# Decoder layer on one core: the feed-forward's first block of rows is split by GpSimd and projected at the end of the cross attention

## The reference, cut to what matters

```python
x = x + attn_ref(layernorm(x), w_qkv, w_out)                    # self attention, 16 heads
x = x + xattn_ref(layernorm(x), ctx, ctx, mask, Wq, bq, ..., Wo, bo)
#   q = query @ Wq.T + bq; softmax over the keys; out @ Wo.T + bo
x = x + ffn_ref(layernorm(x), index_b, index_t, sw1, sb1, ...)
#   shared part: sh = ln(silu(x1) * x2) * g + b; sh @ sw3.T + sb3 for all rows,
#   and one of 8 experts for each of 1024 chosen rows
```

## Time and profile before

| | us |
|---|---|
| median of three runs | 3107.37 |
| lowest and highest | 3104.04, 3114.0 |
| the profiled execution, its time | 3114.0 |
| the profiled execution, its span | 3112.0 |
| TensorE busy in the span | 2916.7 |
| VectorE, ScalarE, GpSimd busy | 2079.8, 1609.6, 1740.0 |
| cross attention ends, feed-forward starts (us from the span's start) | 2617.51 |
| first `up` of the feed-forward | 2639.83 |

### The profile page before, as it was taken

How to read it: one execution, slowest core, us unless ns; L and a number is a source line. 1 busy time by engine, 2 the same in 40 slices (tenths; PEclk the granted TensorE clock), 3 DMA queues, 4 the chain that set the end, 5 groups by cost and what they waited for, 6 DMA issues and landing times. The chain is left out here.

```text
span 3112.0 us, 41615 instructions
## 1 busy us (share of the span) xinstructions
PE 2916.7 (94%) x15224; PEld 1729.4 (56%) x15224; DVE 2079.8 (67%) x3794; ACT 1609.6 (52%) x2998; POOL 1740.0 (56%) x748
## 2 busy tenths in 40 slices
PE   8999799999999999999999999979969997999577
PEld 5888455555555555555555555437855554777533
DVE  4332587777777777777777777635638896677423
ACT  2222066666676666667676767733226674222211
POOL 1000178989898989898989898830020101343366
PEclk9999699999999999999999999989979998999689
DMA  6544835466566565665665656357665563333451
GB/s 224 187 170 155 217 79 119 96 140 130 117 138 130 119 135 112 134 133 113 140 127 119 133 114 144 79 146 210 186 145 141 139 158 115 136 136 109 142 189 40
DMA packets 179536, 427.52 MB, mean 137 GB/s; under 512 B 30189, under 2 KB 51598, under 8 KB 156236
## 3 DMA queue, kind: packets, MB, share of 16 engines
q1 hardware_dynamic: 153158, 275.92, 30.9%
q0 software_dynamic: 24288, 145.27, 23.0%
q10 hardware_dynamic: 1888, 3.67, 0.4%
HBM read 180.69 MB, written 118.79 MB: 96 GB/s over the span
## 5 line engine op out<-in xcount | busy, mean ns | idle before, releaser
L822 DVE TENSOR_REDUCE part_max<-ps_s 128x1 f32<-128x512 f32 x2048 | 1270.5, 684 | 369.6 <-PE ps_s L710 369.4
L924 ACT ACTIVATE probs<-ps_st 128x512 f32<-128x512 f32 x2048 | 1058.6, 603 | 493.0 <-PE ps_st L729 477.9
L657 POOL TENSOR_TENSOR added<-added,probs 128x2048 f32<-128x2048 f32 x251 | 1168.0, 4653 | 72.0 <-ACT probs L924 48.8
L729 PE MATMUL ps_st<-q_stack,k_stack 98*128 98x512 f32 x2048 | 866.6, 426 | 10.1 <-ACT probs L924 8.7
L710 PE MATMUL ps_s<-k_stack,q_stack 96*128 96x512 f32 x2048 | 825.9, 410 | 17.2 <-DMA k_stack<-k_lo 17.2
L729 PEld LDWEIGHTS ps_st<-q_stack,k_stack 98*128 98x128 f32 x2048 | 387.4, 190 | 520.4 <-ACT probs L924 368.7
L740 PE MATMUL ps_pv<-probs,v_sb 128*32 128x512 f32 x4096 | 547.2, 606 | 0.0
L710 PEld LDWEIGHTS ps_s<-k_stack,q_stack 96*128 96x128 f32 x2048 | 396.3, 194 | 111.4 <-DVE part_max L822 30.6
L665 POOL DMA_DIRECT2D probs<-probs x128 | 111.1, 868 | 181.1 <-PE ps_pv L740 176.5
L740 PEld LDWEIGHTS ps_pv<-probs,v_sb 128*32 128x32 f32 x4096 | 80.8, 108 | 162.9 <-ACT probs L924 136.8
L657 POOL TENSOR_TENSOR added<-probs 128x2048 f32<-128x2048 f32 x32 | 146.7, 4586 | 10.6 <-ACT probs L924 10.3
(11 more groups left out here) (294 smaller groups left out, 3709.1 us busy)
## 6 DMA issues: line engine op xcount, KB each, us to landing
probs<-probs POOLq DMA_DIRECT2D x128, 1024.0 KB
q_stack<-q_hi SPq DMA_DIRECT2D x64, 256.0 KB, 6.8
k_stack<-k_hi SPq DMA_DIRECT2D x64, 256.0 KB, 5.9
xq_stack<-q_parts SPq DMA_DIRECT2D x32, 512.0 KB, 5.0
q_parts<-k_stack SPq DMA_DIRECT2D x60, 256.0 KB, 4.2
x_in<-in_x_rows SPq DMA_DIRECT2D x8, 1024.0 KB
q_hi<-qk_h_out SPq DMA_DIRECT2D x8, 1024.0 KB, 4.2
q_lo<-qk_l_out SPq DMA_DIRECT2D x8, 1024.0 KB
```

The lines of the kernel that those rows point to most:

```text
L657: pool.tensor_tensor(added[:, w % 2], left, probs[:, k % RING], ALU.add).then_inc(added_up, 1)
L729: pe.matmul(ps_st[:, n % BANKS], k_stack[0:TOP, w // BPB, j, k * P:(k + 1) * P], q_stack[:, w % 4, j], start=True, stop=True).then_inc(ite ...
L822: dve.tensor_reduce(part_max[:, s:s + 1], ps_s[:, (w * SLOTS + s) % BANKS], AX.X, ALU.max)\
L924: act.activation(probs[:, k % RING, j], ps_st[:, n % BANKS], ACT.Exp, scale=SCALE).then_inc(item_used, 1)
```

## The change

GpSimd takes over the split of the first block (four casts and four subtractions, one for each chunk of 128 x 512) as soon as it is loaded, adds bo to the block's residual rows, and at the end takes the reciprocal square root for two tiles. TensorE makes the first block's 48 projection matmuls at the end of the cross attention, into the banks of `ps_s`. VectorE adds them to `next_x` in place after its last `normalize` and makes the statistics of the first two tiles between those additions. The feed-forward then starts with `norm(0, 0, 0)` and takes the first block's rows from `first_x`. Semaphores that the first block would have raised are raised by hand. bo is loaded at unit 21, and the waits of the start are for the loads that each step needs: `ident_in` for the transposes, `bias_in` for ScalarE. To make room, the second buffer of row maxima (`row_parts`) moves into unused partitions of the `probs` tile.

```diff
@@
-        probs = sb("xprobs", [KH, 2, 2, HEADS, BLK])
+        probs_all = sb("xprobs", [P, 2, 2, HEADS, BLK])
+        probs = probs_all[0:KH]
-        row_parts = [early_rows, sb("xrow_parts", [2 * HEADS, BLK], F32R)[:]]
+        row_parts = [early_rows, probs_all[96:96 + 2 * HEADS, 0, 0, 0].bitcast(F32R)]
...
+                            sp.dma_start(bo_all, bo.partition_broadcast(P)).then_inc(bo_loaded, 16)
...
+                pool.memset(next_half[:], -0.5).then_inc(ones_set, 1)
+                pool.wait_ge(ones_set, 2)
+                pool.wait_ge(next_loaded, 128)
+                for c in range(DC):
+                    pool.tensor_copy(next_h[:, c], ahead_raw[:, c // 2, c % 2]).then_inc(next_high, 1)
+                for c in range(DC):
+                    pool.wait_ge(next_high, c + 1)
+                    pool.tensor_tensor(next_l[:, c], ahead_raw[:, c // 2, c % 2], next_h[:, c].bitcast(F32), ALU.subtract)\
+                        .then_inc(next_low, 1)
+                pool.wait_ge(bo_loaded, 16)
+                for t in range(TPB):
+                    pool.tensor_tensor(next_x[:, t], next_x[:, t], bo_all, ALU.add).then_inc(bo_added, 1)
+                pool.wait_ge(next_eps_added, 1)
+                pool.tensor_tensor(next_rstd[:, 0:2], next_var[:], next_half[:], ALU.pow).then_inc(next_rstd_done, 1)
+                pool.wait_ge(next_rstd_done, 1)
...
+                def project_next(t):
+                    if t == 0:
+                        pe.wait_ge(max_done, UNITS * SLOTS)
+                        pe.wait_ge(next_low, DC)
+                        pe.wait_ge(ahead_low, 2 * len(PARTS))
+                    if t >= BANKS:
+                        pe.wait_ge(next_summed, t - BANKS + 1)
+                    a, w = (next_h, next_l), weights_ahead[0][1:]
+                    for n, (x, y) in enumerate(ORDER):
+                        for c in range(DC):
+                            mm = pe.matmul(ps_s[:, t % BANKS], a[x][:, c, t * P:(t + 1) * P], w[y][:, c],
+                                           start=(n == 0 and c == 0), stop=(n == 2 and c == DC - 1))
+                    mm.then_inc(next_projected, 1)
...
+                for t in range(TPB):
+                    project_next(t)
...
-                    if u == UNITS:
-                        dve.wait_ge(next_high, 1)
-                        dve.tensor_tensor(next_l, ahead_raw[:].rearrange("p a c d -> p (a c) d"), next_h.bitcast(F32), ALU.subtract)\
-                           .then_inc(next_low, 1)
...
+                for t in range(TPB):
+                    dve.wait_ge(bo_added, t + 1)
+                    dve.wait_ge(next_projected, t + 1)
+                    dve.tensor_tensor(next_x[:, t], ps_s[:, t % BANKS], next_x[:, t], ALU.add).then_inc(next_summed, 1)
+                    if t < 2:
+                        dve.wait_ge(next_summed, t + 1)
+                        dve.bn_stats(next_stats[:, t], next_x[:, t]).then_inc(next_stats_done, 1)
+                    if t == 1:
+                        dve.wait_ge(next_stats_done, 2)
+                        dve.sem_inc(next_stats_seen, 1)
+                        for k in range(2):
+                            dve.bn_aggr(next_moments[:, k], next_stats[:, k]).then_inc(next_moments_done, 1)
+                        dve.wait_ge(next_moments_done, 2)
+                        dve.tensor_scalar(next_var[:], next_moments[:, 0:2, 1], EPS, None, ALU.add).then_inc(next_eps_added, 1)
...
-                    if u == UNITS - 1:
-                        act.wait_ge(next_loaded, 128)
-                        act.activation(next_h, ahead_raw[:].rearrange("p a c d -> p (a c) d"), ACT.Copy).then_inc(next_high, 1)
...
-                sp.dma_start(bo_all[:], bo.partition_broadcast(P)).then_inc(bo_loaded, 16)
-                for dst, src in ((ident[:], eye), (bias_raw[:, 0:D], b12.unsqueeze(0)), (bias_raw[:, D:2 * D], b3.unsqueeze(0)),
-                                 (gamma_all[:], gamma.partition_broadcast(P)),
+                sp.dma_start(ident[:], eye).then_inc(ident_in, 16)
+                sp.dma_start(bias_raw[:, 0:D], b12.unsqueeze(0)).then_inc(bias_in, 16)
+                sp.dma_start(bias_raw[:, D:2 * D], b3.unsqueeze(0)).then_inc(bias_in, 16)
+                for dst, src in ((gamma_all[:], gamma.partition_broadcast(P)),
...
-                pool.wait_ge(bo_loaded, 16)
-                add_bias(0, 0)
-                pool.wait_ge(consts, 5)
-                pool.wait_ge(w_loaded, 5 * 16)
-                rsqrt(0, 0, 0)
+                pool.sem_inc(bo_added, TPB)
+                pool.sem_inc(rstd_done, 1)
                 rsqrt(0, 0, 1)
+                pool.wait_ge(w_loaded, 2 * 16)
...
-                residual(0, 0, range(2))
-                residual_stats(0, 0, 0)
-                residual(0, 0, (2,))
+                dve.sem_inc(resid_done, TPB)
+                dve.sem_inc(stats_done, 2)
+                dve.sem_inc(moments_done, 2)
+                dve.sem_inc(eps_added, 1)
+                norm(0, 0, 0)
+                residual_stats(0, 0, 1)
+                norm(0, 0, 1)
                 dve.wait_ge(bias_high, 1)
                 dve.tensor_tensor(bias_rows[32:33], bias_raw[:], bias_rows[0:1].bitcast(F32), ALU.subtract)\
                    .then_inc(bias_low, 1)
-                residual(0, 0, (3,))
-                norm(0, 0, 0)
-                residual_stats(0, 0, 1)
-                norm(0, 0, 1)
...
-                act.wait_ge(w_loaded, 5 * 16)
+                act.wait_ge(bias_in, 2 * 16)
...
-                project(0, 0, range(TPB))
-                pe.wait_ge(w_loaded, 5 * 16)
+                pe.sem_inc(proj_done, TPB)
+                pe.wait_ge(ident_in, 16)
```

More of the change, by code:

```diff
@@ L1280, in cross_attention @@
 def cross_attention(nc, q_parts, xk_parts, xv_rows, pad_row, pad_scaled, mask_q, mask_k, eye, eye_bf, attn_t, weights_ahead,
-                    x1_rows, next_x, next_h, next_l, early, earlier_stored):
+                    x1_rows, next_x, next_h, next_l, bo, bo_all, next_moments, next_rstd, early, earlier_stored):
     HEADS = 4
@@ L1330, in cross_attention @@
         ahead_loaded = [sem(f"xahead_loaded{s}") for s in range(2)]
+        ORDER = ((0, 0), (0, 1), (1, 0))
+        next_stats = sb("xnext_stats", [P, 2, 6])
+        next_var, next_half = sb("xnext_var", [P, 2]), sb("xnext_half", [P, 2])
+        bo_loaded, bo_added, next_projected, next_summed, next_stats_done, next_stats_seen, next_moments_done, next_eps_added = (
+            sem(f"x{n}") for n in ("bo_loaded", "bo_added", "next_projected", "next_summed", "next_stats_done", "next_stats_seen",
+                                   "next_moments_done", "next_eps_added"))
+        next_rstd_done = sem("xnext_rstd_done")
         ahead_high, ahead_low, next_loaded, next_high, next_low = (
@@ L1684, in shared_feed_forward @@
         ones_rows = sb("e_ones_rows", [P, P], F32R)
-        bo_all = sb("bo_all", [P, D])
         gamma_all = sb("e_gamma_all", [P, HF])
@@ L1739, in shared_feed_forward @@
         w_loaded, bias_high, bias_low, consts = (sem(n) for n in ("w_loaded", "bias_high", "bias_low", "consts"))
+        ident_in, bias_in = sem("ident_in"), sem("bias_in")
         loaded = [sem(f"block_loaded{s}") for s in range(2)]
         LOADS = 2
-        bo_loaded, bo_added, a_high, a_low = (sem(n) for n in ("bo_loaded", "bo_added", "a_high", "a_low"))
+        bo_added, a_high, a_low = (sem(n) for n in ("bo_added", "a_high", "a_low"))
         proj_done, resid_done = sem("proj_done"), sem("resid_done")
@@ L1764, in final_pair, with rows_of @@
             return isinstance(i, int) and i == NBLK // 2 - 1
+        def rows_of(i, u):
+            return first_x if first(i, u) else x2[:, u]
         def following(i, u):
@@ L1846, in add_bias @@
                 def add_bias(i, u):
-                    if not first(i, u):
-                        pool.wait_ge(loaded[u], i * (16 * LOADS) + 16 * LOADS * u)
-                    rows = first_x if first(i, u) else x_in[:, u]
+                    pool.wait_ge(loaded[u], i * (16 * LOADS) + 16 * LOADS * u)
+                    rows = x_in[:, u]
                     for t in range(TPB):
-                        pool.tensor_tensor(rows[:, t], rows[:, t], bo_all[:], ALU.add).then_inc(bo_added, 1)
+                        pool.tensor_tensor(rows[:, t], rows[:, t], bo_all, ALU.add).then_inc(bo_added, 1)
                 def z_affine(i, u):
@@ L1937, in residual_stats @@
                         dve.wait_ge(resid_done, count(i, u, TPB, t + 1))
-                        dve.bn_stats(stats[:, t], x2[:, u, t]).then_inc(stats_done, 1)
+                        dve.bn_stats(stats[:, t], rows_of(i, u)[:, t]).then_inc(stats_done, 1)
                     dve.wait_ge(stats_done, count(i, u, TPB, 2 * half + 2))
@@ L1954, in norm @@
                     for t in range(2 * half, 2 * half + 2):
-                        dve.tensor_scalar(h_out[:, u, t], x2[:, u, t], moments[:, t, 0:1], rstd[:, t:t + 1],
```

(10 more changed lines are left out.)

4 lines of the change are left out of this document (1 added, 3 removed).

## The result

| | before | after |
|---|---|---|
| median, us | 3108.49 (4 runs) | 3148.03 (4 runs) |
| lowest and highest | 3104.04, 3114.0 | 3142.16, 3149.72 |
| ratio, 95% interval | | 1.0122 (1.0108 to 1.0135) |

The prediction was 3104.1 with a range to 3110.5. The kernel is 38 us slower by the ratio, and every one of its runs lies outside the range. The profiled execution is the fastest of the four, 3142.16.

A forecast was written before the change was run, and what follows sets the result against it. TensorE was taken as the bound, idle at the seam between cross attention and feed-forward. A restart 4.3 us earlier, less 1.0 for VectorE collisions, gave 3.3 us: 3104.1 from a median of 3107.4, range 3097.4 to 3110.5.

The forecast's parts named there:

- the collision term of the cross attention: Units 21 to 27: GpSimd's 12.7 us of new work disturbs VectorE's `normalize`, costing 1.0 us, bounds 0 and 2.9.
- units of more than 8.26 us near 2550: Sign in the changed trace's cross attention that GpSimd's work disturbs VectorE by more than the 1.0 us taken.
- speaks against this part: Cross attention: two-SBUF-input VectorE instructions and GpSimd SBUF reads exclude each other; 5 us by the rule alone, 1.0 taken.
- Rival D: End of cross attention: clock falls during the 48 projection matmuls, 22 us instead of 11, time 3115.1; chance 0.02.
- stage start: Seam: the projection matmuls and last addition put the feed-forward's start at 2618.8, 1.3 us later than before.
- the residual rows' landing: Feed-forward's start: the second block's load lands 9.3 us after issue, allowing ScalarE's split at T' + 11.7.
- restart: Feed-forward's start: TensorE restarts at 2633.9 instead of 2638.24, 4.3 us gained, bounds 3.8 and 6.2.
- A, "the loads do not bind": Feed-forward's start: VectorE's list sets TensorE's restart at T' + 8.4, a gain of 11.0, time 3097.4; chance 0.08.
- B: Feed-forward's start: third block's loads delay the second's by up to 5.6 us, time 3109.7; chance 0.10.

The follow-up runs named there:

- experiment 5: The changed kernel with each of GpSimd's twelve operations waiting for the semaphore of the one before: 3135.72 us, ratio 1.0083.
- Experiment 4: Kernel before with row maxima moved, plus four, two or one idle VectorE reciprocals (7, 3.5, 1.74 us) before unit 26's row maxima: 3148.25, 3144.18, 3139.43 us.
- paced kernel: The changed kernel with GpSimd's twelve operations dealt out in groups behind `normalize` of units 23 to 26: 3099.54 us, ratio 0.9981 to the kernel before.
- `gaps`: The changed kernel with a semaphore wait between each of GpSimd's twelve operations and the next: 3135.72 us, ratio 1.0083 to the kernel before.
- `dense`: The changed kernel with 16 further TensorE matmuls of 128x128 by 512, results unused, ahead of unit 24's row sums: 3110.18 us, ratio 1.0019.
- `pause1`: The kernel before with row maxima moved and one idle VectorE reciprocal of 1.74 us ahead of unit 26's row maxima: 3139.43 us, ratio 1.0119.
- `splits_only`: The changed kernel with GpSimd's casts and subtractions left back to back and only the bias additions dealt out to later units: 3140.03 us, ratio 1.0112.
- `late`: The changed kernel with GpSimd's whole burst, back to back, started after `normalize` of unit 27: 3098.7 us, ratio 0.9980 to the kernel before.

## Why the prediction was wrong

**The step that failed** is the collision term of the cross attention: "The bounds are nothing (the collisions fall into VectorE's own slack) and 2.9 (three collisions of 0.96, the worst seen). I take 1.0." It measured some 40 us: 5.8 of TensorE's waits (4.75 and 1.06), and for the rest units at half clock. The sign that the prediction named for it, "units of more than 8.26 us near 2550", is in the trace: the stores of units 22 to 25 are 12.9, 15.6 and 14.2 us apart (2541.23, 2554.12, 2569.70, 2583.86). Three things were wrong in it.

- *Which instruction collides.* The term was built on `normalize` alone. The costly one is the cast of the row maxima (`max_rows`), 0.18 us long, for which TensorE waits in `turn_max`. In the kernel before it took at most 0.30 in its 32 times, so no row showed it.
- *How long.* I took a wait for one GpSimd operation. The cast waited 6.77 us, over a rest of subtractions and all four additions. The page of the Trainium skill that the prediction cited (SBUF — State Buffer, "Who interferes with whom") names casts among the instructions that can contend, when their operands meet the conditions of the mode with two ports, which I passed over, and says that the other engine "fully blocks" for the whole instruction. The trace agrees that a cast can be blocked, and shows it blocked for several instructions. With a semaphore wait between the operations it was 1.27, for one (experiment 5).
- *What a late VectorE costs.* I let a delay pass at most one to one. Experiment 4 shows the amplifier: 1.74 us on VectorE cost 1.2%, as much as 7 us. A unit takes 8.26 us at full clock and 14.15 at half (stores at 2583.86 and 2598.01 in the changed kernel); some six units' worth of work was left, so by these rows an estimated 35 us.

The rule that "speaks against this part" was priced at 5 us in the prediction, as four collisions of `normalize`. TensorE's own waits, 5.8 us, are near that price, but by luck: one cast made them, in one collision. The whole price was eight times higher, since neither the rule nor I had the clock in the sum. Rival D named the half clock, but for the projection, which in fact ends it.

**The steps that held.** In the paced kernel, where the disturbance is gone, the seam is as predicted (T' is the feed-forward's start): stage start 12.9 after the last row sums (predicted 12.9); the residual rows' landing 8.9 after issue (9.3), with ScalarE's split released by it at T' + 11.25 (11.7); restart at T' + 14.5 (15.1). From the last row sums to the restart that is 27.4 against 32.3 before, 4.9 gained (4.3 predicted), and the ratio's 5.9 us, 3.1 to 8.7 by its interval, holds both. In the changed kernel itself the clock was at half for the projection's first matmuls, which delays the stage's start to 14.9 after the row sums.

**The rivals.** A, "the loads do not bind", is not what happens, but its sum is right: with the split moved behind the first block's high parts the restart comes at T' + 8.5 (8.4 predicted). B did not show: the third block's loads, issued directly behind, left the second's at 8.9 to 9.0.

**Left open.** Why the cast waited through several GpSimd operations in two kernels (6.77, 6.66) and slipped in after a part of one in two others (0.57) with the operations as close together. It began 3.16 and 3.26 us behind GpSimd's first subtraction in the first two and 3.22 and 3.25 in the others, so its place in the row does not tell them apart. Why the kernel with dense matmuls is 11.8 us and not 3.9 behind the paced one. And why one run of ten in the kernels `gaps` and `dense` went the other way; only the profiled runs have a clock by stretch.

## What to carry to other kernels

Before idle time on one engine is filled, look for the shortest instructions of the engine that shares its way into SBUF, and ask which of them TensorE waits for; a 0.18 us cast was the place. Where TensorE bounds the kernel and its clock is at 1.00, don't price a delay by its length alone: here a wait of 1.1 us cost some 35 us, as the clock fell and stayed. The same work behind the last such dependency cost nothing, with one wait on a semaphore.

## What the runs showed of the hardware that I had not expected

- In the last units of the cross attention the clock stayed where it was, either way: windows with TensorE busy 30.00 of 30.00 us at 0.50 in the changed kernel, 19.78 of 20.00 at 1.00 in the paced one, with the same kinds of matmuls. The projection's matmuls of 128x128 by 512 brought it back some 4 us after they began. The stage's first units, which have further matmuls for the mask, brought it back too: in the changed kernel some 3 us after it had fallen (0.50 from 2324 to 2326, 1.00 from 2328), in the kernel before some 13 us after (0.50 from 2328 to 2340). So a fall need not last; what decides how long it does, no run here shows.
- The clock stood at half 2 to 3 us after a single TensorE wait of 1.14 us (`pause1`) or 1.06 us (`splits_only`). It stayed at 1.00 through 2.09 us of idle time in 16 us that came in waits of at most 0.5 us (`late`).
- VectorE's cast of 128x16 to the rounded format (fp32r) waits for GpSimd's two-input operations, in the worst case for several of them in a row, 6.77 us. Its reciprocals, which have one input, were not held by them: in the changed kernel the 64 of 128x256 took 1.74 us in the median and 1.75 at most.
